# Router products from x1 inside the feed-forward tiles, convolution with x1 stationary, routing under the convolution, whole z rows stored

## What is computed

```python
x  = x + ffn(layernorm(x + proj))      # x1; both weights of ffn ternary, activations quantised
z  = causal_depthwise_conv(x1, w=cond) # 16 taps; tap u of feature d is cond[u, d]
logits = z @ Wr                        # 8 experts
w, sel = top_k(logits, 2); w = softmax(w)
out = x1 + sum_e gate[e] * (z @ We[e] + be[e])
```

## Time and profile before

| | us |
|---|---|
| median of 3 runs | 844.3 |
| lowest and highest run | 838.39, 844.45 |
| span of the profiled execution | 830.2 |
| PE busy in the span | 739.0 |
| DVE, ACT, POOL busy | 560.7, 399.8, 478.7 |

### The profile page before, as it was taken

One profiled execution on the slowest core, in us unless ns is written; L12 is line 12 of the kernel. 1 busy time (PEld: TensorE's weight loads), 2 busy tenths in 40 slices (PEclk: granted clock), 3 DMA queues, 4 the chain that ended last, 5 costly groups with the idle time before them and its releaser, 6 DMA issues.

```text
span 830.2 us, 12602 instructions
## 1 busy us (share of the span) xinstructions
PE 739.0 (89%) x3954; PEld 431.9 (52%) x3954; DVE 560.7 (68%) x832; ACT 399.8 (48%) x636; POOL 478.7 (58%) x738
## 2 busy tenths in 40 slices
PE   1755599999999999999989999929799999999995
PEld 0112244444444444444446663317578888888884
DVE  2469999999999999998636332487463564545452
ACT  2056466667778777776612432414432333343432
POOL 1037889888888888886210000002376887888873
PEclk9986899999999999999999999958899999999998
DMA  9985147799999996554399999999677998999986
GB/s 359 386 324 159 26 89 138 145 180 179 188 181 164 173 191 127 133 115 89 83 219 223 97 103 227 168 100 147 233 125 144 162 169 161 167 166 169 165 160 88
DMA packets 230270, 137.50 MB, mean 166 GB/s; under 512 B 162798, under 2 KB 195054, under 8 KB 229054
## 3 DMA queue, kind: packets, MB, share of 16 engines
q1 hardware_dynamic: 210094, 99.94, 61.5%
q0 software_dynamic: 15456, 36.47, 24.1%
q10 hardware_dynamic: 4656, 0.30, 1.4%
HBM read 80.27 MB, written 35.42 MB: 139 GB/s over the span
## 4 chain that ended last, share of the span: by engine, by line
PE 50%; DMA 12%; SPq 11%; issue 7%; POOL 7%; DVE 6%; ACT 5%; POOLq 0%; DVEq 0%; ACTq 0%
PE PS L1643 21%; PE PS L1532 8%; PE PS L1481 6%; PE PS L1504 5%; PE PS L1493 5%; DMA z_scratch<-ZZ 4%; SPq L557 3%; PE PS L1627 3%; SPq L407 2%; DMA BEB<-in_be 2%; DMA QyT<-Qy 2%; DVE Ih L1117 2%; ACT Qh L844 2%; DMA QT<-Qh 2%; SPq L550 2%
## 5 line engine op out<-in xcount | busy, mean ns | idle before, releaser
L1643 PE MATMUL PS<-W,ZH 128*128 x552 | 179.5, 406 | 4.8 <-DVE ZL L1380 4.1
L768 POOL DMA_INDIRECT ZR<-z_scratch,IDG x69 | 71.7, 1039 | 151.5 <-DVE IDS L1332 130.8
L1481 PE MATMUL PS<-W,QyT 128*128 128x512 bf16 x512 | 124.4, 387 | 27.6 <-DMA QyT<-Qy 16.3
L777 POOL DMA_INDIRECT out_x<-YS,IDS x69 | 109.5, 1587 | 48.4 <-issue 29.2
L1493 PE MATMUL PS<-W,QyT 128*128 128x512 bf16 x512 | 121.1, 379 | 0.0
L971 ACT ACTIVATE YS<-YS,SG 128x512 f32<-128x512 f32 x69 | 50.1, 726 | 146.5 <-DVE YS L1402 140.5
L1504 PE MATMUL PS<-W,QT 128*128 128x512 bf16 x512 | 115.7, 379 | 3.3 <-DMA QT<-Qh 2.4
L1643 PEld LDWEIGHTS PS<-W,ZH 128*128 128x128 f32 x552 | 100.2, 191 | 23.8 <-issue 5.9
L1643 PE MATMUL PS<-W,ZL 128*128 x276 | 109.7, 397 | 0.0
L1380 DVE TENSOR_TENSOR ZL<-PS,ZH 128x512 fp32r<-128x512 f32 x69 | 47.7, 692 | 80.0 <-ACT ZH L960 77.4
L1481 PEld LDWEIGHTS PS<-W,QyT 128*128 128x128 bf16 x512 | 49.5, 99 | 92.3 <-DMA QyT<-Qy 20.0
(11 more groups left out here) (232 smaller groups left out, 1061.5 us busy)
## 6 DMA issues: line engine op xcount, KB each, us to landing
XW<-out_x SPq DMA_DIRECT2D x64, 240.0 KB, 4.7
X<-in_x SPq DMA_DIRECT2D x32, 256.0 KB, 10.0
out_x<-X SPq DMA_DIRECT2D x32, 256.0 KB, 3.7
z_scratch<-ZZ SPq DMA_DIRECT2D x8, 1024.0 KB, 28.9
WRAW<-in_We SPq DMA_DIRECT2D x8, 1024.0 KB, 15.9
XR<-in_x SPq DMA_DIRECT2D x20, 256.0 KB, 4.2
stage<-in_w1T SPq DMA_DIRECT2D x4, 1024.0 KB, 7.8
stage<-in_w2T SPq DMA_DIRECT2D x4, 1024.0 KB, 12.2
```

The lines of the kernel that those rows point to most:

```text
L768: pool.indirect_dma_start(ZR[m % UZ][:], None, z_d, bass.IndirectOffsetOnAxis(IDG[:, m:m + 1].bitcast(U32), 0)) \
L777: pool.indirect_dma_start(x1_d, bass.IndirectOffsetOnAxis(IDS[:, m:m + 1].bitcast(U32), 0), YS[m % UN][:], None, compute_op=ALU.add).then_ ...
L1481: i = nc.tensor.matmul(GP[:, a, :], QyT[t][:, k, :], W12[:, k, o:o + CH], start=(k == 0), stop=(k == KD - 1))
L1643: x = nc.tensor.matmul(bank[i], zz[i % 2][:, k, :], W2[:, bass.ds(q, 1), part, k, :].rearrange("p o d -> p (o d)"), start=(k == 0 and n == ...
```

## The change

- PE turns x1 of tile s-3 between `up(s,0)` and `up(s,1)` (`turn_x1`, 4 transposes) and multiplies it after `up(s,1)` with V (`route`, 4 f32 products, V stationary, 128 columns). V is taps times router, 128 (tap, expert) columns for each of 4 feature blocks, made once on POOL. ACT copies both results (`copy_x1t`, `copy_g`).
- SP stores the 128x128 result skewed by tap (`store_g`) to g_scratch and reads it back by sequence (`load_gs`, pieces of 64 bytes); `pick` (16 products of 8 columns) sums over taps. pick(0) runs in stage 22, pick(1) after convolution group 8.
- The convolution has x1 (XW, 128x128, 128 groups of 16 tokens) stationary and BD moving (128 columns), 32 groups of 4 features, two products each. XW holds x1 once, in pieces of 64 features. BD is zeroed by POOL and DVE and filled by DMA from the taps (`load_bd`, five pieces, pieces of 128 bytes); `spread`, T, `blank` and the router products over z are gone.
- The routing chain, the turning of the last tokens of the groups (straight from ZS, no load ZD) and the tables stand between the convolution groups. After them come dense 0 to 3, then the slots; dense 4 to 7 stand in slots 8 to 11.
- ACT writes z rows of 520 words to ZS, DVE puts the gates in; `store_z` is one transfer for each half (4.26 MB), whole rows. Expert weights are loaded at convolution groups 17 to 31 (0 to 3) and later (4 to 7).

```diff
@@ sync @@
+            def load_late(last):
+                for t in range(TB):
+                    sp.wait_ge(x1_out[t], 16 * last)
+                for j in range(NJ):
+                    for k in (CB - 2, CB - 1):
+                        ...
+                        sp.dma_start(XW[OB * j:OB * j + OB, 1, 1 + k, 0:last - BH, :], ...).then_inc(xw_in[1], 16)
+            def load_bd(i):
+                first, end = PIECES[i]
+                for j in range(NJ):
+                    sp.dma_start(BD[OB * j:OB * j + OB, first:end, j, :, :].rearrange("p i a o -> p i (a o)"), ...).then_inc(bd_in[i], 16)
             def stage(s):
                 if s == NT:
                     sp.wait_ge(u_done, NH * NT)
-                    load_xw(B // 2)
-                    load_xw(B // 2 + 1)
+                    load_late(NT // TB - 2)
+                    sp.wait_ge(bd_zero, 4)
+                    load_bd(1)
                 if tile(s + 1):
                     turn_y(s + 1)
+                if tile(s - 1):
+                    if s == NT:
+                        turn_h(s - 1, 0)
                 if tile(s - 3):
                     store_x1(s - 3)
                 if tile(s - 1):
-                    turn_h(s - 1, 0)
+                    if s < NT:
+                        turn_h(s - 1, 0)
                     turn_h(s - 1, 1)
...
-                if 0 <= s - 6 < NQ * TP:
-                    load_T((s - 6) // TP, (s - 6) % TP)
-                    blank(s - 6)
...
+                if 4 <= s < NT:
+                    b, c = (s - 4) // TB, (s - 4) % TB
+                    load_xw(b, range(NJ // 2 * c, NJ // 2 * c + NJ // 2), 0, CB if b < BH else CB - 2)
+                if tile(s - 4) and s - 4 < NT - 1:
+                    store_g(s - 4)
...
+            store_z(0)
+            sp.wait_ge(z_out[0], 16)
+            sp.wait_ge(zdt_done, 1)
+            load_expert(0)
+            sp.wait_ge(conv_done, NG + 7)
+            load_expert(1)
+            ...
+            sp.wait_ge(conv_done, NG + 15)
+            load_expert(3)
+            store_z(1)
+            sp.wait_ge(tab_done, NK // CC)
+            sp.wait_ge(first_done, 1)
+            load_expert(4)
+            load_expert(5)
+            sp.wait_ge(z_out[1], 16)
+            load_expert(6)
+            load_expert(7)
@@ tensor @@
+            def turn_x1(n):
+                t = n % 2
+                pe.wait_ge(x1_done, n + 1)
+                if n:
+                    pe.wait_ge(g_read, n)
+                ...
+                for k in range(KD):
+                    i = nc.tensor.transpose(X1P[:, P * k:P * k + P], X1[t][:, P * k:P * k + P], IDF[:])
+                i.then_inc(x1t_done, 1)
+            def route(n):
+                ...
+                pe.wait_ge(x1t_read, n + 1)
+                for k in range(KD):
+                    i = nc.tensor.matmul(GP7, V[:, k].rearrange("p u e -> p (u e)"), X1T[:, k, :], start=(k == 0), stop=(k == KD - 1))
+                i.then_inc(g_prod, 1)
+            def conv(r):
+                ...
+                if r >= 4:
+                    pe.wait_ge(z_done, r - 3)
+                for i in range(GI):
+                    for part in range(2):
+                        rows = XW[:, h, 1 - part:1 - part + CB, :, GI * g + i].rearrange("p k b -> p (k b)")
+                        x = nc.tensor.matmul(bank[r % 4][:, P * i:P * i + P], rows, BD[:, GI * g + i, :, 1 - part, :],
+                                             start=(part == 0), stop=(part == 1))
+                x.then_inc(conv_done, 1)
             def stage(s):
                 if tile(s):
...
                     up(s, 0)
+                    if tile(s - 3):
+                        turn_x1(s - 3)
                     up(s, 1)
+                    if tile(s - 3):
+                        route(s - 3)
...
+                if s == NT:
+                    conv(0)
+                    turn_x1(NT - 3)
+                    down(NT - 2)
+                    route(NT - 3)
+                elif s == NT + 1:
+                    turn_x1(NT - 2)
+                    down(NT - 1)
+                    conv(1)
+                    route(NT - 2)
+                elif s == NT + 2:
+                    conv(2)
+                    turn_x1(NT - 1)
+                    conv(3)
+                    route(NT - 1)
+                elif tile(s - 2):
                     down(s - 2)
+                if s == 22:
+                    pick(0)
...
+            for r in range(4, 2 * NG):
+                conv(r)
+                if r == 8:
+                    pick(1)
+                if r == 14:
+                    prefix()
+                if r == 17:
+                    turn_zd()
+                if r in (21, 23, 25, 27):
+                    table((r - 21) // 2)
...
+            for n in range(E // 2):
+                dense(n)
```

More of the change, by code:

```diff
@@ L184, in adaln_ffn_moe @@
         NR = NT * E
[L185 to L191, removed]
+        where = [9, 5, 6, 7, 4, 3, 2, 1]
+        W2 = place("W2", 0, [P, 11, 2, KD, D], F32R)
+        WRAW = [place(f"WRAW{e}", (2 * where[e] + 1) * NEXP, [P, KD, D]) for e in range(E)]
+        assert 2 * where[0] * NEXP == a_h
+        YS = [place(f"YS{i}", D * i, [P, D]) for i in range(UN)]
@@ L192, in adaln_ffn_moe @@
+        ZH = [place(f"ZH{i}", D * (UN + i), [P, KD, P], F32R) for i in range(2)]
+        ZL = [place(f"ZL{i}", D * (UN + 2 + i), [P, KD, P], F32R) for i in range(2)]
+        BEB = place("BEB", 2 * (where[0] + 1) * NEXP, [P, E, D])
         a = a_T + RING * D
-        assert a == 2 * E * NEXP and CC * P <= UN * D and a + UZ * ZW <= a_h
-        AOH = [place(f"AOH{i}", a + CC * P // 2 * i, [P, P, CC], BF16) for i in range(2)]
-        ION = place("ION", a_h, [P, P, CC], BF16)
+        assert a == 2 * (where[3] + 1) * NEXP
@@ new lines, in adaln_ffn_moe @@
+        assert b + 32 <= a_h - 2 * P
+        BOH = [place(f"BOH{i}", a_bd + CC * MT * i, [P, CC, 2, MT], BF16) for i in range(2)]
+        b = a_bd + 2 * CC * MT
+        b2 = (E + 1) * (NT + 1) + 7
+        UPTO = place("UPTO", b, [P, E + 1, NT + 1])
+        WAITS = place("WAITS", b + b2, [P, E, NT], I32)
+        HITS = place("HITS", b + b2 + NR, [P, E, NT])
+        assert b % 8 == 0 and b2 % 8 == 0 and b + b2 + 2 * NR <= a_bd + 3 * GI * 2 * P
+        a = a_h + OB * ZW
+        ION = place("ION", a, [P, P, CC], BF16)
@@ new lines, in stage @@
+                if 6 <= s <= 32 and s % TB == 0 and s != 22:
+                    for b in (BH, BH + 1) if s == 24 else ((s - 6) // TB,):
+                        load_gs(b)
+                if s == NT:
+                    sp.wait_ge(bd_zero, 5)
+                    load_bd(2)
+                if s == NT + 1:
+                    load_xw(B - 2, range(NJ))
+            pipeline(stage)
+            sp.wait_ge(bd_zero, 6)
+            sp.wait_ge(bd_zero_v, 1)
+            load_bd(3)
+            load_gs(B - 2)
@@ L1605, in _, with turn_zd, table @@
+            def turn_zd():
+                pe.wait_ge(z_done, NG)
+                for k in range(KD):
+                    i = nc.tensor.transpose(bank[6][:, P * k:P * k + P], ZS[0][:, ND, P * k:P * k + P], IDF[:])
+                i.then_inc(zdt_done, 1)
+            def table(q):
                 pe.wait_ge(oh_done, q + 1)
```

665 lines of the change are left out of this document (327 added, 338 removed).

## The result

The changed kernel takes **887.7 us** (median of 4 runs, 887.0 to 889.9) against 843.1 us for the kernel before (4 runs, 838.4 to 844.5): ratio **1.055, interval 1.051 to 1.058**. The forecast was 832.5 us, 1.4% faster; it is 5.5% slower, outside the range.

The account below looks back on a forecast made before the run. The prediction took TensorE (PE) as the bound, busy 739.0 of 830.2 us. Its terms, +42.0 + 14.1 - 3.5 - 64.4 = -11.8 us, applied to the median 844.3, gave 832.5 us; range 814 to 854.

Parts of the forecast that it names:

- The price of one f32 matmul record: Tiles and convolution: an f32 record with 128x128 stationary and 128 moving columns costs 0.125 us, bounds 0.110 and 0.144.
- groups of 2.3 us or more: Convolution: sign that the forecast is wrong; a group of 16 records was expected to take 2.0 us.
- Part 1: Router products added inside the tiles, 1.44 us a tile, and pick(0), 3.7 us: +42.0 us up to the end of up(31).
- the 3.5 us of idle time to be had back: First stretches of the tiles: of 3.6 us in which PE idled before, 3.5 are taken off the added router work.
- Part 2: End of the tiles: down(31) waits for QT behind SP's 24 issues; convolution proper starts later, +14.1 us.
- Part 3: Convolution: 448 records at 0.125 plus work moved under it, 65.8 against 69.3 us, -3.5; the routing chain fits, nothing charged.
- Part 4: After the convolution: router products leave the path, z stored at about 400 GB/s, slot 0 at convolution end + 22.5: -64.4 us.
- Weights exposed: Rival: 768 records in convolution and tiles pay for the weight load; 847 us (chance 0.08), 855 and above (0.09).
- Rows of z late: Rival, after the convolution: z's store goes at the old rate, +20 us, 852 us; chance 0.09.
- SP and the DMA engines: Rival, tiles: they bound the tiles, a tile takes 12.8 us instead of 11.8, +28, 860 us; chance 0.12.
- the chain under the convolution: Rival: the routing chain does not fit there, PE waits at the tables and dense, +8, 841 us; chance 0.10.

Follow-up runs that it names:

- e1: A kernel by itself, 64 matmul records of each operand form back to back; contiguous f32 0.112 us a record, stationary stride 64 0.218 us.
- e6: Changed kernel with x1 copied contiguous on POOL, plus SP issuing the late 16 XW loads behind the tiles' last transposes; 842.0 us.
- e9: Changed kernel with contiguous x1 copies (POOL, ACT), z stored in 16 transfers, late XW loads, contiguous second pick, later weight casts; 834.3 us, ratio 1.008.
- e5: Changed kernel with x1 copied contiguous on POOL, plus each half of z stored in 16 transfers of 2080-byte pieces, not one; 843.4 us.
- e2: Changed kernel with the convolution's stationary operand read from 128 contiguous elements of XW, so z is not the convolution; 845.4 us.

## Why the prediction was wrong

**The step that failed is "The price of one f32 matmul record".** It took 0.125 us between bounds of 0.110 and 0.144, and went to the rows "of the same stationary shape". Shape was the wrong likeness. All rows beside it have a contiguous stationary operand; the convolution's has every 64th element, the pick's every 16th. Measured: 0.111 in the tiles, 0.218 in the convolution, 0.21 in the picks. The one row that showed a stride at work was the old convolution's, "slower than its columns", 0.144 against 0.055 that its form takes when contiguous (e1). I saw that it was out of line and put it down to the half-width operand. The sign of being wrong that I had named, groups of 2.3 us or more, came: they take 3.5. The 0.093 us that each strided record was short give: 448 in the convolution 41.7 us, 64 in the tail of the tiles 6.0, 64 in the picks 6.2, together **53.9 of the 67.3 us** by which the sum missed.

**Part 1** was near: 1.33 us a tile against 1.44, 38.6 for 29 tiles. pick(0) cost 6.7 instead of 3.7, and the half clock behind it another 1.7, which the sum did not have. Of the 3.5 us of idle time to be had back only 0.3 showed: T0 moved by 46.7, not 42.0.

**Part 2** was right in its mechanism: down(31) waits behind SP's 24 issues and starts at T0 + 19.3 (T0 + 19 forecast), at half clock. SP's timeline of the changed kernel:

```profile
463.24 7.58 SPq L492 DMA_DIRECT2D XW<-out_x  x16
470.86 3.79 SPq L499 DMA_DIRECT2D BD<-taps_scratch  x8
474.75 1.26 SPq L534 DMA_TRANSPOSE QT<-Qh  x1
```

24 issues in 11.4 us, 0.47 each. The +18.3 instead of +14.1 are the 64 strided records, less 2 us of others. e6 took this wait away and got 5.6 us.

**Part 3**, -3.5 forecast, +40.4 measured: the price, 41.7 + 3.1 for pick(1). Its other claim held: PE is busy for 110.00 of 110 us, so no table waits and the routing chain fits; in e9's convolution of 69 us PE waits for copies alone (7.3 us in all), so it fits there too.

**Part 4** had the right events and two wrong rates. Slot 0 starts at the convolution's end + 33.2, not + 22.5: z's store moved 193 GB/s, not 400 (+9), and the first gather with its landing took 6.5 us beside the next weights. Slots 0 and 1 then take 9.0 us (639.08 to 648.09), where two of 3.20 were counted. -53.9 instead of -67.2. The 400 GB/s were those of the weights *coming in*; no row of before showed long rows going out. e5 shows that the shape of the transfer is part of it (its pieces and its number of issues changed together). What is left in e5, 280 against 400, stays open: the chain names SP's 16 issues, but the DMA engines are busy for 0.96 to 1.00 of the time from 572 to 584 us as well, at 308 to 338 GB/s.

**The rivals.** "Weights exposed" came nearest: 0.22 for a record and 905 us, since it charged the 256 records of the tiles too. Its number for a record was right, its mechanism not: in e1 the load record itself is longer (312 ns against 192), and with only 8 moving columns the pace is the same. The Trainium skill, "TensorE: Matmul & The Clock Gate", "LDWEIGHTS (loading the stationary operand)", has a load cost its columns over 1.2 in ns; for 128 columns that is 107, e1's contiguous 0.112 agrees, and its 0.218 to 0.238 at strides of 4 and above does not. The rule of the Trainium skill's section "The mechanism" on the same page, overlap only across row groups, finds no support: e1 uses one row group throughout, and in its contiguous form (51.1 to 58.2 us) products and loads are both busy all of the time, at 0.112 us a record. "Rows of z late" happened too, at half its price. SP and the DMA engines did not bound the tiles (share 0.78), and the chain under the convolution held.

Corrected in that one price, the sum gives 832.5 + 53.9 = 886.4 us. That it meets 887.7 owes something to luck: the other terms missed 13.4 us more, and the span of before on which the sum was made lies 14.1 us below its median, while the changed kernel's lies only 2.0 below.

## What to carry to other kernels

Before an f32 operand of a matmul is priced from a neighbouring row, compare its element stride as well as its shape: here a stationary operand with a stride of 4 elements or more, or a moving one with a stride of 64, doubled the record from 0.11 to 0.22 us, and making the operand contiguous by copies on an engine that is idle in that stretch gave back 40 of 888 us. When a row is slower than its columns explain, find out why before the change multiplies it. Moving work out of a stage in which PE waits into one in which it is full costs all of it: even with the stride gone, 29 tiles paid 38.6 us for the router and the first pick, still strided, 8.4, nearly all of the 50 us saved behind the convolution. And a price per record belongs to a granted clock: read the two together before two forms are compared.

## What the runs showed of the hardware that was not expected

- f32 stationary operands with strides of 4, 8, 16, 17, 64 and 65 elements all cost 0.218 to 0.238 us a record, stride 2 only 0.119: a step, not a slope. A moving operand at stride 64 costs 0.219; one in runs of 16 elements with gaps costs nothing extra (0.112).
- The strided records do not feel the granted clock: 0.22 us at 1.00 and at 0.50 (e1 L102; the changed kernel behind pick(1)). Contiguous ones do: in e2 96 of them take 13.4 us where the clock is 0.50 for the first 5.3, against 0.114 each at 1.00. By these numbers a contiguous record at 0.50 costs about 0.21, nearly as much as a strided one (an estimate: 8.1 us at 0.114 are 71 records, which leaves 25 for the 5.3 us).
- The granted clock fell from 1.00 to 0.50 while PE was busy without a gap, in every run of products with 8 moving columns (both picks of the changed kernel, e1 L102). It came back behind the picks, under bf16 and f32 matmuls of 512 and 128 columns.
- Two column tiles of 64 columns do run at the same time: contiguous records alternate at 0.055 us (e1 L96), half of 0.112. At moving stride 64 it is 0.146 (L99), so a pair takes 0.29, more than the one full-width strided record with 0.22.
- A store of 33 KB rows in one transfer was slower (193 GB/s) than the same bytes in 16 transfers of 2 KB rows (280 GB/s).
